# Routed expert blocks: the plain fp32 slice split like the others, half of a subtraction on GpSimd, four weight buffers

## The reference, cut to what matters

```
scores = sigmoid(x @ gate_w.T) + bias
topk_w, topk_idx = top_k(scores, 4); topk_w /= sum(topk_w)
g = x @ Wg[e].T ; u = x @ Wu[e].T          # for every expert e
out += (silu(g) * u * weight_of(e)) @ Wd[e].T
out += silu(x @ Sg.T) * (x @ Su.T) @ Sd.T  # one shared expert
```

## Time and profile before

| | |
|---|---|
| median of 3 runs | 1274.57 us (1273.64 to 1277.37) |
| profiled execution, its own time | 1276.3 us |
| its span, first to last instruction | 1274.5 us |
| TensorE busy | 1097.4 us (86%) |
| VectorE busy | 905.9 us (71%) |
| ScalarE busy | 704.8 us (55%) |
| GpSimd busy | 566.7 us (44%) |
| routed blocks, first layer | about 79 to 333 us of the span |
| routed blocks, second layer | about 793 to 1046 us of the span |

### The profile page before, as it was taken

One profiled execution on the slowest core, in us unless ns is written; L12 is line 12 of the kernel. 1 busy time (PEld: TensorE's weight loads), 2 busy tenths in 40 slices (PEclk: granted clock), 3 DMA queues, 4 the chain that ended last, 5 costly groups with the idle time before them and its releaser, 6 DMA issues. The chain is left out here.

```text
span 1274.5 us, 21579 instructions
## 1 busy us (share of the span) xinstructions
PE 1097.4 (86%) x5654; PEld 717.9 (56%) x5655; DVE 905.9 (71%) x1775; ACT 704.8 (55%) x1218; POOL 566.7 (44%) x582
## 2 busy tenths in 40 slices
PE   4969999999194899999997787999999947878597
PEld 3847777777182233333333675677777735467454
DVE  5869888887575888888860666888888847444632
ACT  3238787887143177777775131787888824424142
POOL 4335666664556244443331225566666545140200
PEclk9979999999596599999998888999999977989889
DMA  9367899764615550000000183789995561000001
GB/s 351 114 220 185 218 243 286 174 114 60 192 50 155 104 99 19 1 1 1 1 1 1 63 309 111 236 196 258 275 222 103 83 156 67 1 1 1 0 1 66
DMA packets 62798, 151.01 MB, mean 118 GB/s; under 512 B 12224, under 2 KB 17024, under 8 KB 58240
## 3 DMA queue, kind: packets, MB, share of 16 engines
q1 hardware_dynamic: 37440, 95.17, 22.3%
q0 software_dynamic: 22592, 50.27, 20.3%
q10 hardware_dynamic: 2688, 4.65, 1.1%
HBM read 104.89 MB, written 44.97 MB: 118 GB/s over the span
## 5 line engine op out<-in xcount | busy, mean ns | idle before, releaser
L811 POOL DMA_INDIRECT moe_acc_rows<-xn,moe_token_of x94 | 208.0, 2213 | 146.3 <-ACT xn L886 131.1
L923 DVE TENSOR_TENSOR moe_w_lo<-moe_raw,moe_w_hi 128x1536 fp32r<-128x1536 f32 x94 | 165.4, 1759 | 62.9 <-ACT moe_w_hi L874 62.7
L1977 ACT ACTIVATE causal_prob<-causal_sc 128x512 f32<-128x512 f32 (+3 forms) x384 | 166.8, 492 | 70.3 <-PE causal_sc L1882 69.7
L874 ACT CAST moe_w_hi<-moe_raw 128x1536 fp32r x94 | 138.7, 1475 | 78.0 <-issue 76.4
L1864 PE MATMUL causal_mx<-ks,causal_qs 96*128 (+4 forms) x384 | 131.4, 353 | 23.0 <-DMA causal_qs<-causal_parts 16.5
L831 PE MATMUL moe_gu<-moe_w_hi,xt_hi 128*128 128x512 f32 x282 | 148.4, 526 | 0.6 <-DVE moe_w_lo L923 0.6
L1882 PE MATMUL causal_sc<-causal_qs,ks 99*128 (+3 forms) x384 | 120.2, 333 | 1.9 <-ACT causal_prob L1977 1.7
L831 PE MATMUL moe_gu<-moe_w_hi,xt_lo 128*128 128x512 f32 x282 | 111.8, 396 | 0.0
L831 PE MATMUL moe_gu<-moe_w_lo,xt_hi 128*128 128x512 f32 x282 | 110.9, 393 | 0.0
L826 PE MATMUL moe_gu<-moe_raw,xn 128*128 x188 | 98.0, 603 | 5.0 <-ACT moe_w_hi L874 5.0
L1808 POOL TENSOR_SCALAR_AFFINE_SELECT causal_prob<-causal_prob 128x512 f32<-128x512 f32 x64 | 40.9, 639 | 115.9 <-ACT causal_prob L1977 115.5
(11 more groups left out here) (317 smaller groups left out, 2724.5 us busy)
## 6 DMA issues: line engine op xcount, KB each, us to landing
moe_raw<-in_w_gu SPq DMA_DIRECT2D x34, 1024.0 KB, 6.1
moe_raw<-in_w_down SPq DMA_DIRECT2D x34, 512.0 KB, 8.2
causal_qs<-causal_parts SPq DMA_DIRECT2D x45, 128.0 KB, 3.6
moe_acc_rows<-moe_zeros SPq DMA_DIRECT2D x2, 2304.0 KB, 14.7
moe_acc_rows<-x SPq DMA_DIRECT2D x18, 256.0 KB, 2.0
moe_xn_rows<-xn SPq DMA_DIRECT2D x2, 2048.0 KB, 10.7
x<-moe_acc_rows SPq DMA_DIRECT2D x16, 256.0 KB, 6.8
xn<-moe_acc_rows ACTq DMA_DIRECT2D x16, 256.0 KB, 7.2
```

Of the source, the lines that this page charges most:

```text
L811: pool.indirect_dma_start(acc_rows[a], bass.IndirectOffsetOnAxis(ap=token_of[:, b - 3:b - 2].bitcast(U32), axis=0), out_rows[(b - 3) % OUT ...
L874: nc.scalar.copy(w_hi[1 - s][:, :, :], raw[:, bass.ds(at + SPLIT_AT, GU_COLS - SPLIT_AT)].rearrange("p (k n) -> p k n", k=SPLIT)).then_inc ...
L923: nc.vector.tensor_tensor(w_lo[1 - s][:, :, :], raw[:, bass.ds(at + SPLIT_AT, GU_COLS - SPLIT_AT)].rearrange("p (k n) -> p k n", k=SPLIT), ...
L1977: nc.scalar.activation(prob[u % 2][:, h, o:CH], sc[(u * QPK + h) % BANKS][:, o:CH], ACT.Exp, scale=SCALE).then_inc(exp_done, 1)
```

## The change

All four slices of gate/up are split. On TensorE slice 0 becomes three f32r matmuls, so 12 instead of one fp32 and nine f32r; the order within a slice is now hi·hi, lo·hi, hi·lo (tokens·weights), and only the first matmul that needs w_lo waits for it. On ScalarE w_hi takes 2048 instead of 1536 columns and xt_hi 512 instead of 384; on VectorE w_lo and xt_lo grow likewise and the copy L937 goes. Of the down weights' lo, VectorE makes one half (512 of 1024 columns) and GpSimd the other. GpSimd loads the weights' place into a register for it, and does it between the gather and the scatter of the same step. The down product waits for both halves, and so does the refill of weights, in place of gate/up. RAW is 4 instead of 5; small maps of the routing, which used a raw buffer's space, get space of their own.

```diff
-RAW = 5
+RAW = 4
 EARLY = 3
-PLAIN = 1
-SPLIT = KT - PLAIN
...
                 end = sp.value_load(first_of[0:1, bass.ds(e - RAW + 1, 1)], min_val=0, max_val=NB)
                 sp.wait_ge(lo_down, end)
-                sp.wait_ge(gu_done, end)
+                sp.wait_ge(lo_down_pool, end)
...
                     pool.indirect_dma_start(rows[n % RING][:, :], None, xn_rows, bass.IndirectOffsetOnAxis(
                         ap=token_of[:, n:n + 1].bitcast(U32), axis=0)).then_inc(gathered[n % RING], 16)
+                if there(b + 1):
+                    at = pool.value_load(raw_at[0:1, b + 1:b + 2], min_val=0, max_val=(RAW - 1) * W_COLS)
+                    pool.wait_ge(hi_down, b + 2)
+                    nc.gpsimd.tensor_tensor(down_lo[(b + 1) % 4][:, 1, :], raw[:, bass.ds(at + GU_COLS + H, H)],
+                                            down_hi[(b + 1) % 4][:, 1, :].bitcast(F32), ALU.subtract).then_inc(lo_down_pool, 1)
                 if there(b - 3):
...
-                    for k in range(PLAIN):
-                        nc.tensor.matmul(gu[s][:, :], xt_plain[s][:, k, :], raw[:, bass.ds(at + k * 2 * FI, 2 * FI)],
-                                         start=(k == 0), stop=False)
-                    pe.wait_ge(lo_gu, b + 1)
-                    for k in range(PLAIN, KT):
-                        for half, part in ((m.xt_hi, w_hi), (m.xt_hi, w_lo), (m.xt_lo, w_hi)):
-                            last = nc.tensor.matmul(gu[s][:, :], xt(half, s, k), part[s][:, k - PLAIN, :], start=False,
-                                                    stop=(k == KT - 1 and half is m.xt_lo))
+                    for k in range(KT):
+                        for half, part in ((m.xt_hi, w_hi), (m.xt_lo, w_hi), (m.xt_hi, w_lo)):
+                            if k == 0 and part is w_lo:
+                                pe.wait_ge(lo_gu, b + 1)
+                            last = nc.tensor.matmul(gu[s][:, :], xt(half, s, k), part[s][:, k, :],
+                                                    start=(k == 0 and half is m.xt_hi and part is w_hi),
+                                                    stop=(k == KT - 1 and part is w_lo))
...
                     pe.wait_ge(lo_down, b - 1)
+                    pe.wait_ge(lo_down_pool, b - 1)
...
-                    nc.scalar.copy(w_hi[1 - s][:, :, :], raw[:, bass.ds(at + SPLIT_AT, GU_COLS - SPLIT_AT)].rearrange(
-                        "p (k n) -> p k n", k=SPLIT)).then_inc(hi_gu, 1)
+                    nc.scalar.copy(w_hi[1 - s][:, :, :], raw[:, bass.ds(at, GU_COLS)].rearrange(
+                        "p (k n) -> p k n", k=KT)).then_inc(hi_gu, 1)
...
-                    nc.vector.tensor_tensor(down_lo[(c + 1) % 4][:, :, :], raw[:, bass.ds(at + GU_COLS, W_COLS - GU_COLS)].rearrange(
-                        "p (i h) -> p i h", i=IT), down_hi[(c + 1) % 4][:, :, :].bitcast(F32), ALU.subtract).then_inc(lo_down, 1)
+                    nc.vector.tensor_tensor(down_lo[(c + 1) % 4][:, 0, :], raw[:, bass.ds(at + GU_COLS, H)],
+                                            down_hi[(c + 1) % 4][:, 0, :].bitcast(F32), ALU.subtract).then_inc(lo_down, 1)
...
-                    nc.vector.tensor_copy(xt_plain[s][:, :, :], tx[s][:, 0:PLAIN * P].rearrange("p (k c) -> p k c", k=PLAIN)).then_inc(tx_plain, 1)
```

More of the change, by code:

```diff
@@ L291, in moe_layer @@
             spare = raw[:, EARLY * W_COLS:RAW * W_COLS].bitcast(BF16)
+            block_maps = sb("block_maps", [P, 3 * T * TOPK * NB], BF16)
             beats = spare[:, 0:T * E * E].rearrange("p (t a b) -> p t a b", t=T, a=E)
@@ L313, in moe_layer @@
             at_place = spare[:, at:at + n_place].rearrange("p (t r c) -> p t r c", t=T, r=TOPK)
-            at += n_place
-            in_block, in_block_p, in_block_t = (spare[:, at + n * n_block:at + (n + 1) * n_block].rearrange(
+            in_block, in_block_p, in_block_t = (block_maps[:, n * n_block:(n + 1) * n_block].rearrange(
                 "p (t r c) -> p t r c", t=T, r=TOPK) for n in range(3))
@@ L701, in routed_blocks @@
         rows += [sb(f"rows{s}", [P, ROW])[:, :] for s in range(len(rows), RING)]
-        xt_plain = [xn_half[:, IN_XN * ROW + s * PLAIN * P:IN_XN * ROW + (s + 1) * PLAIN * P].rearrange("p (k c) -> p k c", k=PLAIN)
-                    for s in range(2)]
-        w_hi = [sb(f"w_hi_{s}", [P, SPLIT, 2 * FI], F32R) for s in range(2)]
-        w_lo = [sb(f"w_lo_{s}", [P, SPLIT, 2 * FI], F32R) for s in range(2)]
+        w_hi = [sb(f"w_hi_{s}", [P, KT, 2 * FI], F32R) for s in range(2)]
+        w_lo = [sb(f"w_lo_{s}", [P, KT, 2 * FI], F32R) for s in range(2)]
         def down_buffers(half, early, at):
@@ L724, in routed_blocks @@
         raw_ready, act_go = sem("raw_ready"), sem("act_go")
-        hi_gu, hi_down, lo_gu, lo_down = sem("hi_gu"), sem("hi_down"), sem("lo_gu"), sem("lo_down")
+        hi_gu, hi_down, lo_gu, lo_down, lo_down_pool = sem("hi_gu"), sem("hi_down"), sem("lo_gu"), sem("lo_down"), sem("lo_down_pool")
         gathered, gathered_start = gathered
         scattered, scattered_start = zip(*[m.gpsimd_dma_semaphore(f"scattered{a}", 16 * len(range(a, NB, 2))) for a in range(2)])
-        tx_done, tx_hi, tx_plain, tx_lo = sem("tx_done"), sem("tx_hi"), sem("tx_plain"), sem("tx_lo")
+        tx_done, tx_hi, tx_lo = sem("tx_done"), sem("tx_hi"), sem("tx_lo")
         gu_done, silu_done, z_done = sem("b_gu_done"), sem("b_silu_done"), sem("b_z_done")
@@ L731, in routed_blocks @@
         y_done, y_out = sem("b_y_done"), sem("y_out")
-        SPLIT_AT = PLAIN * 2 * FI
         def there(b):
@@ L750, in xt, with tokens @@
             return half[:, k, s * P:(s + 1) * P]
-        def halves(s):
-            return slice(PLAIN, KT), slice(s * P, (s + 1) * P)
+        def tokens(s):
+            return slice(s * P, (s + 1) * P)
         block = ctx.enter_context(nc.Block())
@@ L895, in step @@
                         act.wait_ge(gu_done, b + 1)
-                    ks, tokens = halves(s)
-                    nc.scalar.copy(m.xt_hi[:, ks, tokens], tx[s][:, PLAIN * P:KT * P].rearrange("p (k c) -> p k c", k=SPLIT)).then_inc(tx_hi, 1)
+                    nc.scalar.copy(m.xt_hi[:, :, tokens(s)], tx[s][:, :].rearrange("p (k c) -> p k c", k=KT)).then_inc(tx_hi, 1)
                 if there(b - 1):
@@ L922, in step @@
                     dve.wait_ge(hi_gu, b + 2)
-                    nc.vector.tensor_tensor(w_lo[1 - s][:, :, :], raw[:, bass.ds(at + SPLIT_AT, GU_COLS - SPLIT_AT)].rearrange(
-                        "p (k n) -> p k n", k=SPLIT), w_hi[1 - s][:, :, :].bitcast(F32), ALU.subtract).then_inc(lo_gu, 1)
+                    nc.vector.tensor_tensor(w_lo[1 - s][:, :, :], raw[:, bass.ds(at, GU_COLS)].rearrange(
+                        "p (k n) -> p k n", k=KT), w_hi[1 - s][:, :, :].bitcast(F32), ALU.subtract).then_inc(lo_gu, 1)
                     dve.wait_ge(hi_down, b + 2)
-                    nc.vector.tensor_tensor(down_lo[(c + 1) % 4][:, :, :], raw[:, bass.ds(at + GU_COLS, W_COLS - GU_COLS)].rearrange(
-                        "p (i h) -> p i h", i=IT), down_hi[(c + 1) % 4][:, :, :].bitcast(F32), ALU.subtract).then_inc(lo_down, 1)
+                    nc.vector.tensor_tensor(down_lo[(c + 1) % 4][:, 0, :], raw[:, bass.ds(at + GU_COLS, H)],
+                                            down_hi[(c + 1) % 4][:, 0, :].bitcast(F32), ALU.subtract).then_inc(lo_down, 1)
                 if there(b):
@@ L934, in step @@
                 if there(b + 2):
-                    ks, tokens = halves(s)
                     dve.wait_ge(tx_hi, b + 3)
-                    nc.vector.tensor_copy(xt_plain[s][:, :, :], tx[s][:, 0:PLAIN * P].rearrange("p (k c) -> p k c", k=PLAIN)).then_inc(tx_plain, 1)
-                    nc.vector.tensor_tensor(m.xt_lo[:, ks, tokens], tx[s][:, PLAIN * P:KT * P].rearrange("p (k c) -> p k c", k=SPLIT),
-                                            m.xt_hi[:, ks, tokens].bitcast(F32), ALU.subtract).then_inc(tx_lo, 1)
+                    nc.vector.tensor_tensor(m.xt_lo[:, :, tokens(s)], tx[s][:, :].rearrange("p (k c) -> p k c", k=KT),
+                                            m.xt_hi[:, :, tokens(s)].bitcast(F32), ALU.subtract).then_inc(tx_lo, 1)
                 if there(b - 1):
```

2 lines of the change are left out of this document (removed).

## The result

| | before | changed |
|---|---|---|
| median of 4 runs | 1275.14 us (1273.64 to 1277.37) | 1356.33 us (1354.69 to 1359.68) |
| profiled execution, span | 1274.5 us | 1355.5 us |

The changed kernel takes 1.0639 of the time, interval [1.0611, 1.0666]: 81 us more, where 28 were forecast. The direction and the range held, the likeliest case did not.

What follows compares the result with a forecast made beforehand. TensorE, dense at 4.99 us a block, was taken to bound the kernel, with ScalarE becoming the pace. Terms 18 + 3 - 1 + 6 + 2 = 28 us on 1276.3 gave 1304, as the runs' median 1303 us; range 1287 to 1405.

Steps and rivals of the forecast that it cites:

- the likeliest case: Routed blocks: ScalarE becomes the pace, 1303 us in all, its own range 1287 to 1335 us, chance 0.50.
- the largest term: The 18 us forecast for ScalarE's longer w_hi and xt_hi in the routed blocks.
- ScalarE as the pace: Routed blocks: wider w_hi and xt_hi make ScalarE's block 5.12 to 5.25 us, above TensorE's 4.82; 18 us more.
- ScalarE's least block is the sum of its work: ScalarE, routed blocks: 4.58 us is the least, nothing hides added work, so 0.43 and 0.11 us add in full.
- No wait but the one for its registers: ScalarE's timeline before: its 4.58 us catch-up block was read as containing no wait except for its registers.
- GpSimd's subtraction: Half of down lo on GpSimd: 1.29 us a block, taking turns with VectorE's subtractions; 6 us, bounded at 17 to 26.
- the second rival: "GpSimd behind by a little", routed blocks: stops without the chain, 5.6 to 6.0 us a block, 1335 to 1370 us; chance 0.12.
- The locked chain: First rival: GpSimd falls behind, a two-block chain through ScalarE closes at 6.65 us a block, 1400 us; chance 0.28.
- Fill and tail: Layer starts, where longer w_hi and w_lo are unhidden, cost 3 us; last blocks, TensorE alone, give back 1 us.
- Buffers: Weight loads with four raw buffers instead of five: only runs of short experts drain them; 2 us, bounds 0 and 10.
- TensorE's block: TensorE, routed blocks: three f32r matmuls replace the plain one, 0.17 us less, 4.82 us a block.
- says otherwise: GpSimd's gather of 2.55 us beside w_lo was taken to contradict the inference that descriptor generation is left alone.

Runs made afterwards that it cites:

- e2: The kernel before with four raw buffers instead of five, the routing's maps in space of their own: 1278.61 us, ratio 1.0021.
- e1: The changed kernel with all of the down weights' low part on VectorE, no GpSimd subtraction or waits for it: 1274.78 us, ratio 0.9978.
- e10: The changed kernel with GpSimd's subtraction replaced by one equally long fill of unused memory, that low part left out: 1280.64 us, ratio 1.0034.
- e8: e1 with TensorE's eight gate/up products on w_hi first and the four on w_lo last: 1263.21 us, ratio 0.9908 to the kernel before.
- e4: The changed kernel with five raw buffers, w_lo and down buffers placed differently to make room: 1357.22 us, ratio 1.0615.

## Why the prediction was wrong

Its mechanism for the largest term failed, and the case that came was a rival with a chance of 0.12.

*ScalarE as the pace, 18 us: false.* The durations were right (w_hi 1.908 us, xt_hi 0.59). The step that failed is the sentence that "ScalarE's least block is the sum of its work", with 4.58 us for it, in which the 0.75 us ahead of w_hi are counted as work. "No wait but the one for its registers" misread the row: the earlier trace rows put these 0.75 us down to SPq, a wait for SyncE, and only the 0.88 us of the next block to issue. The same work takes 3.71 us in e2, and 3.71 + 0.43 + 0.11 = 4.25 us is what the changed kernel shows, 4.24 with no gap: the two additions were right, and the base was 0.87 us too large. The gap that rows do put down to issue shrinks with the pace too, from 0.81 us a block before to 0.43 in e1 at 4.79 us a block, so it was slack. That the register loads lie under queued work or under a wait that the row doesn't name would explain it; no run shows it. By e1 the term is 0.

*GpSimd's subtraction, 6 us: the mechanism was right, the size off; it measured 76 us by e10 and 82 by e1.* The prediction found the turns in the earlier trace rows and bounded them at 17 to 26 us by VectorE's block, 4.13 + 1.29. Two things were missing. It priced what VectorE loses, not what GpSimd loses next: its scatter then falls under the delayed w_lo (3.46 us for 1.55). And it compared GpSimd's 4.36 us with ScalarE's supposed 5.12 to 5.25, where TensorE's was 4.80, so 0.44 us of room were taken for 0.76 to 0.9. The result is nearest to the second rival, "GpSimd behind by a little": 5.6 to 6.0 us a block and 1335 to 1370 us forecast (0.63 to 1.03 us on 86 blocks give 1329 to 1364), 5.6 us a block over the two layers (5.81 and 6.07 in the two stretches) and 1356 us measured. That its numbers fit is in part luck: it put stops of 0.7 to 1.3 us on 4.9 us of work, and it was 4.36 us of work and stops of 1.2 us by the mean, 1.5 and 1.7 in the stretches.

*The locked chain, 6.65 us a block from the sixth on: half right.* The late stretch settles at 6.2 us, L884 waits for scatters there and y for the subtraction. But what closes without slack is GpSimd's own cycle of three instructions and two gaps, not the two-block path through ScalarE, and it holds steadily only from block 35 of the second layer; before that, intervals of 4.2 to 12.2 us alternate. The scatter's 3.46 us in this cycle depend on where w_lo falls, and w_lo waits for ScalarE; no run takes these two apart.

*Fill and tail, +3 and -1: too small.* e1 has TensorE's 0.17 to 0.19 us a block (15 us in 86) and ends 1 us ahead of before, so about 14 us are lost elsewhere: 5.1 and 4.9 us in the first four blocks of the two layers and 4.8 us at the late refill. e8, which hides w_lo at the start, gets 12 us back.

*Buffers, 2 us: right* for the kernel before (2.7 us, e2), about 4.8 us in e1, and no gain from a fifth in the change (e4). *TensorE's block, 4.82: right* (4.79).

The Trainium skill (SBUF — State Buffer, Who interferes with whom) says that a VectorE instruction with two on-chip inputs and a GpSimd instruction that reads that memory lock each other out for the whole instruction. The runs agree: 3.83 us of w_lo are 0.40 + 1.28 + 2.15. Its inference that such a tensor_tensor leaves GpSimd's descriptor generation alone can't be used for these transfers: with no GpSimd subtraction at all, e10's scatters still take 2.07 us by the mean, where those that meet no w_lo take 1.59. Whether they are stopped in making descriptors or in reading their row numbers (token_of), which lie in the same memory, no run here separates, so the prediction's "says otherwise" was too strong.

What stays open: how the first layer's irregular intervals arise one by one, and what ends the gap ahead of w_hi, which the rows call issue.
